# GpSimd multiplies the own rows of the node stages, and SP begins the stores of their tiles

## The chip, the cores and the metric

The kernel runs on one NeuronCore of one Trainium2 chip. The metric is the device time of one execution in microseconds; a lower one is better. The engines are named as in the profile: PE (TensorE, the matrix engine), DVE (VectorE), ACT (ScalarE), POOL (GpSimd) and SP (SyncE, which only begins transfers here). Each engine runs its own list of instructions in order; they meet at semaphores.

## The reference, cut to what matters

One layer of a graph network over 6250 nodes with 256 features, beside a linear attention over the same rows, and then a mixture of experts. The graph part has three GAT layers over 200,000 edges and a loop at every node (its own edge):

```
xn = layernorm(x)
for layer in 0, 1, 2:
    xh = (h @ W).reshape(n, heads, d)
    a_s, a_d = (xh * att_src).sum(-1), (xh * att_dst).sum(-1)
    alpha = leaky_relu(a_s[src] + a_d[dst], 0.2)      # edges and own loops
    alpha = softmax of alpha over the edges that end in dst
    out = segment_sum(xh[src] * alpha, dst) + bias
    h_new = layernorm(out) * g + b
    if layer > 0: h_new = h_new + h
    h = relu(h_new)
x = x + h + mix(xn)
x = x + experts(layernorm(x))
```

For a node, the loop's part of `out` is `xh[node] * alpha_own`: one row times one softmax weight per head. The edges' part comes from the sums that an edge stage has left in `acc`.

## The kernel before, in words

The program is a row of phases with a barrier of all engines between them: `prepare_walk` (lists of edges), `turn_weights`, then `node_phase` 0, `edge_phase` 0, `node_phase` 1, `edge_phase` 1, `node_phase` 2, `edge_phase` 2, and then `final_phase` and `experts`. The change touches `node_phase` alone, which `build` calls three times (stages 0, 1 and 2 below, by its argument `layer`). An edge stage lies between two node stages and takes over 2 ms.

A node stage works on 49 tiles (`NB`) of 128 nodes, over rings of four buffers (`TILE_RING`). For tile b in stages 1 and 2:

- SP loads the tile's projected rows (`rows`, 128x260) from memory, and in stage 2 also the previous h (`prev`). It waits for `h_ready` of tile b - 4 before (L565), which frees the buffers.
- DVE, in `gather_in`: `O = rows * own weight` (L660), `acc = acc * edge weight` (L662), `O = O + acc` (L665), `bn_stats` (L668), `bn_aggr` (L671). ACT takes the square root of the variance (L736, `std`).
- DVE, in `finish`: reciprocal (L681), (O - mean) * g (L691), * rstd + b (L695), and in stage 2 max(prev, 0) + O (L704). The last of them writes `Hn` and raises `h_ready`.
- PE transposes Hn (L793) and then projects the tile before it (L802, L803: five matmuls, two k steps of fp32 in two passes each and one bias). ACT copies the transposed tile (L747, `hT`) and takes the projection out of PSUM (L758 to L760, `extend`), and in stages 1 and 2 clears the tile's `acc` (L763).
- POOL waits for `h_ready` and stores Hn to memory (L584), waits for `ext_ready` and stores `ext` (L586), in that order, tile by tile.

In stage 0 there are no own rows: `X` is loaded and normalized (L668, L671, L681, L689).

DVE's order is written out by `step`: for tile b it takes turns between `gather_in` of tile b + 1 and `finish` of tile b, one instruction of each. So before the change the order on DVE is: L660, L681, L662, L691, L665, L695, L668, (L704), L671. Semaphore waits lie between them, as the dependences ask. ACT's order in step b is L736 of tile b + 1, L747 of tile b, L758 to L763 of tile b - 1. PE's order in step b is L793 of tile b, L802 and L803 of tile b - 1. Before it writes Hn, DVE waits until the store of Hn four tiles earlier has landed (`h_out`, L686); ACT does so for `ext` (`ext_out`, L756). At the end of the stage POOL waits for all stores.

Of the kernel before, what the change touches and what calls it, by code (L numbers as in the profile page):

```python
# [17 lines left out]
ALU = mybir.AluOpType  # L18
# [3 lines left out]
P = 128  # L22
# [3 lines left out]
NB = -(-N // P)  # L26
TAIL = N - (NB - 1) * P
NPAD = NB * P
H = 4
# [405 lines left out]
def padded_ring_rows(dram, i, slot):  # L435
    return dram[bass.ds((TILE_RING * i + slot) * P, P), :]
# [6 lines left out]
def node_phase(nc, layer, st, io, dr):  # L443
# [8 lines left out]
    with Phase(nc, f"node{layer}") as ph:  # L452
# [56 lines left out]
        hT_ready = ph.sem("hT_ready")  # L509
        projected = ph.sem("projected")  # L510
        ext_ready = ph.sem("ext_ready")
        h_out = [ph.sem(f"h_out{k}") for k in range(TILE_RING)]
        ext_out = [ph.sem(f"ext_out{k}") for k in range(TILE_RING)]
        block = ph.block()
# [13 lines left out]
        @block.sync  # L528
        def _(sp):
            if not first:  # L530
                for n, name in enumerate(("ln_g", "ln_b")):
                    sp.dma_start(vecs[:, n, :], broadcast_row(io[f"{name}{layer - 1}"])).then_inc(vecs_in, 16)
            sp.dma_start(W[:, :, :], W_dram.rearrange("(k p) o -> p k o", p=P)).then_inc(weights_in, 16)
            sp.wait_ge(bias_clear, 2)
            sp.dma_start(head_view(bias[:, 0:RW]), io[f"bias{layer}"].rearrange("(a h f) -> a h f", a=1, h=H)
                         .broadcast_to([3, H, D])).then_inc(bias_in, 16)
            sp.wait_ge(att_clear, 1)
            for n, a in enumerate((a_src, a_dst)):
                if heads == H:
                    for h in range(H):  # L540
                        o = (h * D) % P
                        sp.dma_start(att[o:o + D, h * D // P, n * H + h:n * H + h + 1],
                                     a[h:h + 1, :].rearrange("a d -> d a")).then_inc(weights_in, 16)
                else:

                    for k in range(2):
                        for h in range(H):
                            sp.dma_start(att[:, k, n * H + h:n * H + h + 1],
                                         a[0:1, k * P:(k + 1) * P].rearrange("a d -> d a")).then_inc(weights_in, 16)

            def load(i, slot, last):
                n = slice(0, TAIL) if last else slice(0, P)
                if first:
                    sp.dma_start(X[n, slot, :], ring_rows(io["x"], i, slot, last)).then_inc(loaded[slot], 16)
                if not first:
                    sp.dma_start(rows[:, slot, :], padded_ring_rows(dr["rows"], i, slot)).then_inc(loaded[slot], 16)
                if layer >= 2:
                    sp.dma_start(prev[:, slot, :], padded_ring_rows(dr["h"], i, slot)).then_inc(loaded[slot], 16)

            for slot in range(TILE_RING):  # L560
                load(0, slot, False)
            with sp.Fori(1, NB // TILE_RING) as i:
                for slot in range(TILE_RING):

                    sp.wait_ge(h_ready, TILE_RING * (i - 1) + slot + 2)  # L565
                    load(i, slot, False)
            sp.wait_ge(h_ready, NB - TILE_RING + 1)
            load(NB // TILE_RING, 0, True)

        @block.gpsimd  # L570
        def _(g):
# [6 lines left out]
            if first:  # L578
                g.memset(acc[:, :, :], 0.0).then_inc(consts, 1)

            def step(i, slot, last):
                b = TILE_RING * i + slot
                g.wait_ge(h_ready, b + 2)
                g.dma_start(padded_ring_rows(dr["xn" if first else "h"], i, slot), Hn[:, slot, :]).then_inc(h_out[slot], 16)  # L584
                g.wait_ge(ext_ready, b + 3)
                g.dma_start(padded_ring_rows(dr["rows"], i, slot), ext[:, slot, :]).then_inc(ext_out[slot], 16)  # L586

            over_ring(g, step)
            for slot in range(TILE_RING):
                n = NB // TILE_RING + (slot == 0)  # L590
                g.wait_ge(h_out[slot], 16 * n)
                g.wait_ge(ext_out[slot], 16 * n)

        @block.vector
        def _(v):
# [26 lines left out]
            if not first:  # L622
# [16 lines left out]
                for k in range(2):  # L639
                    c0.add(v.tensor_tensor(es[:, k, :, :], es[:, k, :, :], zr[:, :, :], ALU.mult))  # L640
                c0.wait()
                v.wait_ge(vecs_in, 32)

            N1 = 1 if first else 4
            N2 = 1 if first else 2 + (layer >= 2)

            def gather_in(i, slot, last):
# [6 lines left out]
                else:  # L654
                    o = O[:, slot, :]
                    oh = by_head(o)
                    a = acc[:, bass.ds(b, 1), 0:RW].rearrange("p a (h f) -> p (a h) f", h=H)[:, :, 0:D]
                    e, z = (es[:, k, bass.ds(b, 1), :].rearrange("p a h -> p (a h)").unsqueeze(2).broadcast_to([P, H, D])
                            for k in range(2))
                    ch.add(v.tensor_tensor(oh, head_view(rows[:, slot, :]), e, ALU.mult))  # L660
                    yield
                    ch.add(v.tensor_tensor(a, a, z, ALU.mult))  # L662
                    yield
                    ch.wait()
                    ch.add(v.tensor_tensor(oh, oh, a, ALU.add))  # L665
                    yield
                    ch.wait()
# [1945 lines left out]
```

## Time and profile before

| | |
|---|---|
| median of 3 runs | 7856.95 us |
| lowest and highest | 7854.21 and 7859.71 us |
| the profiled execution, its own time | 7847.88 us |
| its span, first to last instruction | 7846.2 us |
| PE busy | 4723.7 us (60%) |
| DVE busy | 5395.1 us (69%) |
| ACT busy | 1840.4 us (23%) |
| POOL busy | 5214.3 us (66%) |

The page gives the busy time of each engine over the whole span. Most of it is that of the three edge stages. The three node stages take some 110, 170 and 185 us with their starts and ends, so the shares of the page say little on them, and the trace is asked stage by stage. Stage 0 lies at about 125 to 240 us of the span, stage 1 at 2387 to 2564, stage 2 at 4700 to 4892. PEclk, the granted TensorE clock, is 0.5 at 1.2 GHz and 1.0 at 2.4 GHz; a value between them is a mean over both.

### The profile page before, as it was taken

To read this page: it belongs to the slowest core of one execution; us is meant where nothing else is said; L and a number is where in the kernel's file an instruction comes from. 1 tells how busy PE (TensorE), PEld (TensorE's weight loads), DVE (VectorE), ACT (ScalarE), POOL (GpSimd) and SP (SyncE) were. 2 spreads that over 40 slices of the span, in tenths; PEclk is the share of its full clock that TensorE was granted. 3 is DMA by queue.
4 is the path that set the end of the run, shared out by engine and by line. 5 is a ranking of instruction groups with operands and counts; after the bars stand their busy time and mean duration, and the time that the engine had idled before them with its cause. 6 is when DMAs were issued, how large, how long until landed. Compare 5 with 4: busy or idle time off the path is not lost. (4 is left out here: it accounts for less than half of the span.)

```text
span 7846.2 us, 112094 instructions
## 1 busy us (share of the span) xinstructions
PE 4723.7 (60%) x22712; PEld 3574.8 (46%) x22713; DVE 5395.1 (69%) x14589; ACT 1840.4 (23%) x6460; POOL 5214.3 (66%) x5539
## 2 busy tenths in 40 slices
PE   3466666656656366666655556466666655553686
PEld 2344444444444244444444443355555544432575
DVE  4477777777768477777777667577777776678333
ACT  1211111111103122222211104133333311114454
POOL 3677777777772777777777753777777777743333
PEclk7688888777777688888877775788888877775898
DMA  3555555555553455555544434455555544436333
GB/s 103 160 165 167 170 170 169 163 164 165 164 146 100 134 146 149 149 146 146 147 141 137 136 95 143 141 152 154 154 149 153 152 141 138 135 103 197 66 57 78
DMA packets 544968, 1106.94 MB, mean 141 GB/s; under 512 B 129378, under 2 KB 337743, under 8 KB 544227
## 3 DMA queue, kind: packets, MB, share of 16 engines
q0 software_dynamic: 274368, 731.65, 34.4%
q1 hardware_dynamic: 268883, 368.24, 15.1%
q8 instruction: 168, 2.75, 0.1%
q14 instruction: 397, 3.25, 0.1%
q10 hardware_dynamic: 1152, 1.05, 0.0%
HBM read 960.64 MB, written 148.65 MB: 141 GB/s over the span
## 5 line engine op out<-in xcount | busy, mean ns | idle before, releaser
L1108 POOL DMA_INDIRECT edges_G<-rows,edges_index x4980 | 4747.3, 953 | 1550.7 <-issue 1472.3
L1302 PE MATMUL edges_ps_o<-edges_G,edges_OH 128*128 128x264 f32 x9960 | 3211.9, 475 | 2262.9 <-DVE acc L1566 2259.5
L1302 PEld LDWEIGHTS edges_ps_o<-edges_G,edges_OH 128*128 128x128 f32 x9960 | 2211.7, 236 | 2969.8 <-DVE acc L1566 1774.7
L1548 DVE TENSOR_TENSOR edges_G<-edges_G,edges_ps_c 128x1024 f32<-128x1024 f32 x1245 | 1502.7, 1207 | 0.2 <-issue 0.2
L1566 DVE TENSOR_TENSOR acc<-acc,edges_ps_o 128x264 f32 x2490 | 1052.2, 423 | 244.6 <-DVE acc L1566 142.8
L1447 DVE TENSOR_TENSOR edges_tu<-edges_ad,edges_G 128x80 f32<-128x80 f32 x249 | 74.9, 301 | 1448.7 <-DMA edges_G<-rows,edges_index 1448.7
L1540 DVE TENSOR_TENSOR edges_OH<-edges_ps_c,relT 128x512 f32<-128x512 f32 x1245 | 844.6, 679 | 1.2 <-issue 0.6
L1145 ACT ACTIVATE edges_fade<-edges_ps_s 128x4 f32<-128x4 f32 x249 | 43.2, 174 | 2796.3 <-PE edges_ps_s L1269 2710.9
L1127 ACT ACTIVATE edges_node<-terms 128x12 bf16 x2490 | 476.5, 209 | 178.4 <-issue 124.1
L2382 POOL DMA_INDIRECT x<-experts_Y,experts_token x105 | 170.2, 1621 | 351.8 <-DVE experts_token L2517 218.5
L1135 ACT ACTIVATE edges_ps_c<-edges_diff 128x80 f32<-128x80 f32 x249 | 60.0, 241 | 1262.5 <-DVE edges_diff L1528 1261.3
L1434 DVE TENSOR_SCALAR edges_OHT<-edges_rels,lane 128x1280 bf16<-128x1280 bf16 x498 | 260.9, 566 | 0.0
L2407 PE MATMUL experts_psH<-experts_xs,experts_Wup 128*128 128x128 f32 x1680 | 213.5, 281 | 66.8 <-DVE experts_Wup L2497 65.8
L2407 PEld LDWEIGHTS experts_psH<-experts_xs,experts_Wup 128*128 128x128 f32 x1680 | 198.6, 193 | 101.5 <-issue 78.2
L586 POOL DMA_DIRECT2D rows<-node_ext x147 | 80.2, 545 | 212.8 <-ACT node_ext L760 174.5
L802 PE MATMUL node_psB<-node_Wx,node_hT 128*128 128x264 f32 x588 | 219.7, 512 | 0.0
L1260 PEld LDWEIGHTS edges_ps_s<-edges_node,edges_OHT 128*128 128x128 bf16 x4980 | 161.2, 96 | 118.9 <-issue 59.2
L1974 POOL DMA_INDIRECT xslot<-final_XH,final_slots x98 | 99.1, 1011 | 172.2 <-DVE final_slots L2154 144.1
L1260 PE MATMUL edges_ps_s<-edges_node,edges_OHT 128*128 128x12 bf16 x4980 | 161.7, 168 | 79.0 <-DVE edges_OHT L1434 63.3
L2416 PE MATMUL experts_psY<-W,experts_hT 128*128 x840 | 198.6, 379 | 0.1
L1289 PEld LDWEIGHTS edges_ps_s<-edges_dropped,edges_front 128*128 128x128 f32 x498 | 155.6, 313 | 50.1 <-issue 3.5
L2497 DVE COPY experts_Wup<-W 128x1024 f32 x105 | 94.7, 902 | 114.4 <-issue 71.6
(342 smaller groups left out, 6192.9 us busy)
## 6 DMA issues: line engine op xcount, KB each, us to landing
edges_rels<-rel SPq DMA_DIRECT2D x249, 640.0 KB
edges_G<-rows,edges_index POOLq DMA_INDIRECT x4980
xslot<-edges_blank SPq DMA_DIRECT2D x80, 650.0 KB
edges_masks<-lanes SPq DMA_DIRECT2D x249, 96.0 KB
rows<-node_ext POOLq DMA_DIRECT2D x147, 130.0 KB, 2.3
experts_X<-xslot SPq DMA_DIRECT2D x105, 130.0 KB, 2.1
node_rows<-rows SPq DMA_DIRECT2D x98, 130.0 KB, 2.1
edges_xm<-xn SPq DMA_DIRECT2D x98, 128.0 KB
```

Of the source, the lines that this page charges most:

```text
L802: pe.matmul(psB[slot % 2][:, 0:RW + H], hT[:, slot % TILE_RING, k, :], Wx[:, k, :], start=(k == 0), stop=False)
L1108: g.indirect_dma_start(G[n][:, s, 0:RW], None, dr["rows"], bass.IndirectOffsetOnAxis(index[n][:, s:s + 1], 0)).then_inc(gathered[n], 16)
L1127: ins = a.activation(node[n][:, g, :], terms[:, bass.ds(b, 1), :, :].rearrange("p a h k -> p (a h k)"), ACT.Copy)
L1260: mm = pe.matmul(ps_ad[:, s * KEPT:(s + 1) * KEPT], OHT[:, s, :], node[n][:, s // 2, :], start=True, stop=True)
L1302: mm = pe.matmul(ps_o[BANK_OF[g]][:, 0:GW], OH[:, 2 * g + j, :], G[n][:, 2 * g + j, :], start=(j == 0), stop=(j == 1))
L1434: v.tensor_scalar(OHT[:, s, :].rearrange("p s e -> p (s e)"), rels[:, c * WG * P:(c + 1) * WG * P], lane[:, 0:1], None, ALU.is_equal).then ...
L1540: v.tensor_tensor(OH[:, 4 * k:4 * k + 4, :], ps_iota.unsqueeze(1).broadcast_to([P, 4, P]), rel.unsqueeze(2).broadcast_to([P, 4, P]), ALU.i ...
L1548: v.tensor_tensor(g4[:, :, :, 0:D], g4[:, :, :, 0:D], ps_w[:, 4 * k:4 * k + 4, :].unsqueeze(3).broadcast_to([P, 4, H, D]), ALU.mult).then_ ...
L1566: v.tensor_tensor(a, a, ps_o[BANK_OF[g]][:, 0:GW], ALU.add).then_inc(added, 1)
L2382: g.indirect_dma_start(dr["x2"], bass.IndirectOffsetOnAxis(token[:, slot, :], 0), Y[:, slot, :], None, compute_op=ALU.add).then_inc(y_out, 16)
L2407: mm = pe.matmul(psH[slot % 2][:, c * P:(c + 1) * P], Wup[:, slot % 2, k, c * P:(c + 1) * P], xs[:, slot % 2, k, :], start=(k == 0), stop= ...
L2416: mm = pe.matmul(psY[slot % 2][:, 0:C], hT[:, slot % 2, c * P:(c + 1) * P], W2[:, bass.ds(e, 1), c, :].rearrange("p a o -> p (a o)"), star ...
```

## The change

DVE's first multiplication, L660, goes. In its place POOL computes the same product for every tile of stages 1 and 2, ahead of DVE by up to four tiles. It waits for the own weights once (`shares_ready`), and for each tile for its load and for the buffer O. DVE waits for POOL's result (`owned`) before the addition of L665. The stores of Hn and of ext go from POOL's queue to SP's, in all three stages. SP's loop over the tiles is written out, 49 tiles in straight line, with the store of ext two tiles behind: store Hn of b, load tile b + 4, store ext of b - 2. POOL's list is written out too. What SP and POOL wait for at the end of the stage moves to SP.

```diff
+            def store_h(b):
+                sp.wait_ge(h_ready, b + 2)
+                sp.dma_start(dr["xn" if first else "h"][b * P:(b + 1) * P, :], Hn[:, b % TILE_RING, :]).then_inc(h_out[b % TILE_RING], 16)
+
+            def store_rows(b):
+                sp.wait_ge(ext_ready, b + 3)
+                sp.dma_start(dr["rows"][b * P:(b + 1) * P, :], ext[:, b % TILE_RING, :]).then_inc(ext_out[b % TILE_RING], 16)
+
...
-            with sp.Fori(1, NB // TILE_RING) as i:
-                for slot in range(TILE_RING):
-
-                    sp.wait_ge(h_ready, TILE_RING * (i - 1) + slot + 2)
-                    load(i, slot, False)
-            sp.wait_ge(h_ready, NB - TILE_RING + 1)
-            load(NB // TILE_RING, 0, True)
+            for b in range(NB):
+                store_h(b)
+                if b + TILE_RING < NB:
+                    load((b + TILE_RING) // TILE_RING, b % TILE_RING, b + TILE_RING == NB - 1)
+                if b >= 2:
+                    store_rows(b - 2)
+            for b in (NB - 2, NB - 1):
+                store_rows(b)
+            for slot in range(TILE_RING):
+                n = NB // TILE_RING + (slot == 0)
+                sp.wait_ge(h_out[slot], 16 * n)
+                sp.wait_ge(ext_out[slot], 16 * n)
...
-            def step(i, slot, last):
-                b = TILE_RING * i + slot
-                g.wait_ge(h_ready, b + 2)
-                g.dma_start(padded_ring_rows(dr["xn" if first else "h"], i, slot), Hn[:, slot, :]).then_inc(h_out[slot], 16)
-                g.wait_ge(ext_ready, b + 3)
-                g.dma_start(padded_ring_rows(dr["rows"], i, slot), ext[:, slot, :]).then_inc(ext_out[slot], 16)
...
+            def weigh_own(b):
+                slot = b % TILE_RING
+                g.wait_ge(loaded[slot], 16 * loads * (b // TILE_RING + 1))
+                if b >= TILE_RING:
+
+                    g.wait_ge(h_ready, b - TILE_RING + 2)
+                g.tensor_tensor(by_head(O[:, slot, :]), head_view(rows[:, slot, :]),
+                                es[:, 0, b, :].unsqueeze(2).broadcast_to([P, H, D]), ALU.mult).then_inc(owned, 1)
+
+            if not first:
+                g.wait_ge(shares_ready, 1)
+                for b in range(NB):
+                    weigh_own(b)
...
                 c0.wait()
+                v.sem_inc(shares_ready, 1)
                 v.wait_ge(vecs_in, 32)
 
-            N1 = 1 if first else 4
+            N1 = 1 if first else 3
...
-                    e, z = (es[:, k, bass.ds(b, 1), :].rearrange("p a h -> p (a h)").unsqueeze(2).broadcast_to([P, H, D])
-                            for k in range(2))
-                    ch.add(v.tensor_tensor(oh, head_view(rows[:, slot, :]), e, ALU.mult))
-                    yield
+                    z = es[:, 1, bass.ds(b, 1), :].rearrange("p a h -> p (a h)").unsqueeze(2).broadcast_to([P, H, D])
                     ch.add(v.tensor_tensor(a, a, z, ALU.mult))
                     yield
                     ch.wait()
+                    v.wait_ge(owned, b + 1)
                     ch.add(v.tensor_tensor(oh, oh, a, ALU.add))
```

By the taking of turns in `step`, the order on DVE becomes: L662, L681, L665, L691, L668, L695, L671, (L704).

## Rows read from the trace of the kernel before

**Rows 1.** Instructions that write Hn, by tile; first and last start in us.

```profile
L689 DVE TENSOR_SCALAR node_Hn<-node_X,node_mv,node_rstd x49: 410/413/509, 144.3 to 231.4; 128x256 f32<-128x256 f32 x49
L695 DVE SCALAR_TENSOR_TENSOR node_Hn<-node_O,node_rstd,node_vecs x49: 475/479/485, 2410.2 to 2546.7; 128x256 f32<-128x256 f32 x49
L704 DVE SCALAR_TENSOR_TENSOR node_Hn<-node_prev,node_O x49: 402/407/424, 4723.6 to 4875.3; 128x256 f32<-128x256 f32 x49
```

**Rows 2.** Windows, stages 1 and 2: us; busy PE, PEld, DVE, ACT, POOL; PEclk, DMA, GB/s.

```profile
2413.00:2545.00 132.00, 100.91 (x322) 60.88 (x323) 117.85 (x370) 63.39 (x276) 48.57 (x90) 0.71 0.43 135
4727.00:4873.00 146.00, 118.85 (x322) 69.09 (x322) 128.24 (x413) 63.82 (x273) 48.55 (x90) 0.57 0.51 161
```

**Rows 3.** Timeline, stage 1, DVE: start us, duration us, engine, line, operation [idle before].

```profile
2436.21 0.18 DVE L671 BATCH_NORM_AGGREGATE node_mv<-node_stats 128x2 f32<-128x6 f32 x1
2436.37 0.43 DVE L660 TENSOR_TENSOR node_O<-node_rows,node_es 128x256 f32<-128x256 f32 x1
2436.75 0.16 DVE L681 RECIPROCAL node_rstd<-node_sd 128x1 f32<-128x1 f32 x1
2436.91 0.42 DVE L662 TENSOR_TENSOR acc<-acc,node_es  x1
2437.25 0.48 DVE L691 SCALAR_TENSOR_TENSOR node_O<-node_O,node_mv,node_vecs 128x256 f32<-128x256 f32 x1
...
2437.98 0.48 DVE L695 SCALAR_TENSOR_TENSOR node_Hn<-node_O,node_rstd,node_vecs 128x256 f32<-128x256 f32 x1
2438.37 0.42 DVE L668 BATCH_NORM_STATS2 node_stats<-node_O 128x6 f32<-128x256 f32 x1
2438.93 0.18 DVE L671 BATCH_NORM_AGGREGATE node_mv<-node_stats 128x2 f32<-128x6 f32 x1
```

**Rows 4.** Timeline, stage 1, a chain from one square root to the next but one.

```profile
2482.88 0.29 ACT L736 ACTIVATE node_sd<-node_mv,node_eps 128x1 f32<-128x1 f32 x1
...
2483.21 0.16 DVE L681 RECIPROCAL node_rstd<-node_sd 128x1 f32<-128x1 f32 x1 [0.41 <-ACT node_sd L736]
...
2484.44 0.48 DVE L695 SCALAR_TENSOR_TENSOR node_Hn<-node_O,node_rstd,node_vecs 128x256 f32<-128x256 f32 x1
...
2484.97 0.69 PE L793 MATMUL node_psA<-ident,node_Hn 128*128 128x128 f32 x2 [0.35 <-DVE node_Hn L695]
...
2487.35 0.40 PE L803 MATMUL node_psB<-node_bias,node_ones 3*128 3x264 bf16 x1
...
2488.62 0.29 ACT L736 ACTIVATE node_sd<-node_mv,node_eps 128x1 f32<-128x1 f32 x1
```

**Rows 5.** Timeline, stage 2, DVE: from the reciprocal to Hn.

```profile
4799.86 0.16 DVE L681 RECIPROCAL node_rstd<-node_sd 128x1 f32<-128x1 f32 x1
...
4801.82 0.41 DVE L704 SCALAR_TENSOR_TENSOR node_Hn<-node_prev,node_O 128x256 f32<-128x256 f32 x1
```

**Rows 6.** Timeline at the start of stage 0: a POOL and a DVE instruction.

```profile
125.75 10.87 POOL L579 MEMSET acc<- 128x12936 f32 x1
...
128.40 8.38 DVE L601 CAST node_parts<-node_bias 3x264 bf16<-3x264 f32 x1 [4.11 <-DMA node_bias<-in_L_gnn_bias]
136.81 0.42 DVE L603 TENSOR_TENSOR node_bias<-node_bias,node_parts 3x264 f32<-3x264 f32 x1
```

**Rows 7.** Waits in stage 0, 145 to 233 us: total us, times, longest.

```profile
DVE node_Hn L689 <- DMA xn<-node_Hn: 3.7, 8, 1.3
```

**Rows 8.** DMA issues: queue, count, KB each, median us from issue to landing.

```profile
rows<-node_ext POOLq DMA_DIRECT2D x147, 130.0 KB, 2.3
...
x<-final_Hn SPq DMA_DIRECT2D x49, 128.0 KB, 1.7
```

**Rows 9.** Timeline at the end of stage 2: the last ext and its store.

```profile
4879.95 0.39 ACT L760 ACTIVATE node_ext<-node_psB 128x260 f32<-128x260 f32 x1
...
4880.84 0.54 POOL L586 DMA_DIRECT2D rows<-node_ext  x1
```

**Rows 10.** Timeline, stage 2, SP's queue: two loads behind each other.

```profile
4724.24 0.35 SPq L556 DMA_DIRECT2D node_rows<-rows  x1
4724.77 0.34 SPq L558 DMA_DIRECT2D node_prev<-h  x1
```

More of the change, by code:

```diff
@@ L511, in node_phase @@
         ext_ready = ph.sem("ext_ready")
+        shares_ready = ph.sem("shares_ready")
+        owned = ph.sem("owned")
         h_out = [ph.sem(f"h_out{k}") for k in range(TILE_RING)]
@@ L579, in _ @@
                 g.memset(acc[:, :, :], 0.0).then_inc(consts, 1)
-            def step(i, slot, last):
-                b = TILE_RING * i + slot
-                g.wait_ge(h_ready, b + 2)
-                g.dma_start(padded_ring_rows(dr["xn" if first else "h"], i, slot), Hn[:, slot, :]).then_inc(h_out[slot], 16)
-                g.wait_ge(ext_ready, b + 3)
-                g.dma_start(padded_ring_rows(dr["rows"], i, slot), ext[:, slot, :]).then_inc(ext_out[slot], 16)
[L588 to L592, printed above, removed]
+            def weigh_own(b):
[9 more added lines that the diff above has]
+                    weigh_own(b)
         @block.vector
```

## Prediction

> **What bounds the kernel now.** The page says little here, since the change lies in three short stages. I first asked when Hn is written: first and last start over 48 steps give a tile every (231.4 - 144.3)/48 = 1.815 us in stage 0, 2.844 in stage 1 and 3.160 in stage 2 [rows 1]. All of the change's steady part is 49 tiles times a difference of such periods; 1% of a stage is 1.4 us of 7857, so even a large gain is small.
>
> Then the windows: in stage 1 DVE is busy 117.85 of 132 us, but PE too is busy 100.91, and the granted clock is 0.71, so 42% of the time lies at 2.4 GHz and 58% at 1.2. In stage 2 it is 0.57: 14% and 86% [rows 2]. So two limits have to be worked out for each stage, one per clock level.
>
> The first is DVE's own list. In a stretch where it never waits, one tile goes from L671 to L671 in 2.72 us [rows 3]. The reader is to see that an instruction begins before the one ahead has ended: a tensor_tensor of 0.42 us takes a place of 0.34 us, a scalar_tensor_tensor of 0.48 takes 0.39, L681 and L671 0.16 each. Stage 2 has L704 besides, which fills most of the 0.56 us that DVE otherwise spends from L668 to L671: some 2.82 us, an estimate.
>
> The second is a chain through three engines, at 1.2 GHz. ACT works in order, so the square root of tile b + 3 stands behind taking out and clearing tile b, that waits for PE's projection of b, which stands behind the transposes of b + 1, and these wait for Hn of b + 1, so for the square root of b + 1. The rows show it: square root at 2482.88, reciprocal at 2483.21, Hn done at 2484.92, PE from 2484.97 to 2487.75, the square root but one at 2488.62 [rows 4]. That is 0.33 + 1.71 + 0.05 + 2.78 + 0.87 = 5.74 us for two tiles, 2.87 each, which is the period of stage 1 as measured. With stage 2's 2.37 us from reciprocal to Hn done [rows 5] in the place of 1.71 it is 6.40, 3.20 each. At 2.4 GHz PE's 2.78 would be about half (an estimate), the chain 4.35, 2.2 each, and DVE bounds. So 0.58/2.87 + 0.42/2.72 gives 2.81 us a tile in stage 1 and 0.86/3.20 + 0.14/2.82 gives 3.14 in stage 2, within 0.04 us of the measured periods.
>
> **The multiplication leaves DVE.** What goes is a place of 0.38 us [rows 3], and the new order also puts L695 between L668 and L671, where DVE waited. New list: L662 0.34, L681 0.16, L665 0.34, L691 0.39, L668 0.34, L695 0.39, L671 0.16, together 2.12; the square root between L671 and L681 takes some 0.6 and only 0.50 covers it, so 2.22. That is 0.50 less than 2.72. In stage 2 L704 covers the square root: 2.45.
>
> But the chain doesn't get shorter in stage 1. From reciprocal to Hn there were L681, L662, L691, L665, L695; now there are L681, L665, L691, L668, L695: again 1.71. At 1.2 GHz the period stays 2.87, and the freed 0.65 us become DVE idle. In stage 2 L704 now waits only for L695: 0.16 + 0.34 + 0.39 + 0.34 + 0.53 + 0.41 = 2.17 for 2.37, the chain 6.20, 3.10 each.
>
> **The multiplication on POOL.** The trace has no such instruction on POOL. The nearest row is the memset, 10.87 us for 12936 elements, 0.84 ns each [rows 6], 0.22 us for 256. A product reads twice and writes once; if these passes follow each other it is 0.65 us (an estimate). I take that; the ends are 0.22 and twice 0.65. POOL has one of them per tile and no stores any more, so it isn't the bound. Its result comes in time: SP begins the load of tile b + 4 some 0.5 us after Hn of b, it lands about 2 us later, plus 0.65, while DVE wants it three rounds of over 2.2 us later.
>
> The question is what it does to DVE. While the memset runs, DVE's L601, a cast of three partitions, lasts 8.38 us, and DVE goes on 0.19 us after the memset's end [rows 6]. So a POOL instruction can keep a DVE instruction out for its whole length. L601 has one input; whether L662, L665, L691 and L695, with two inputs from SBUF, are kept out no row shows. I take it that they are (bounds: nothing, and the full hold per tile). Of 0.65 us about 0.2 then lie beside L668, L671 and L681, and 0.45 delay DVE where it has no idle time. At 2.4 GHz stage 1 goes to 2.22 + 0.45 = 2.67 from 2.72, stage 2 to 2.90 from 2.82. At 1.2 GHz the hold falls into the freed 0.65 us of idle: nothing. It comes there by timing too: it starts some 2.7 us after Hn of b, close behind Hn of b + 1, when DVE is soon to wait for the square root. Stage 1: 0.58/2.87 + 0.42/2.67 is 2.78, less 0.02 x 49 = 1 us. Stage 2: 0.86/3.10 + 0.14/2.90 is 3.07, less 0.07 x 49 = 3.5 us.
>
> The Trainium skill (SBUF — State Buffer, "SBUF: two separate sides") says that GpSimd and VectorE share one pair of ports as an exclusive lock for a whole instruction, and that an operation of VectorE with two SBUF inputs takes it against one of GpSimd that reads SBUF. The trace agrees as far as the 8.38 us of L601 go; for two inputs no run here shows it. By that rule the sum is the one above; without it, it is that of the first rival. The GPSIMD Engine Reference ("Elementwise — side-by-side cycle accounting") of the same skill gives about 2.6 cycles an element for this operation, 0.6 us for 256 by an estimate from it, and advises VectorE for it.
>
> **The start of stages 1 and 2.** POOL can start four tiles at once, 2.6 us of holds while DVE begins: about 1 us each, +2 us; ends 0 and +5.
>
> **The stores go to SP.** POOL stored Hn of b + 1 behind ext of b, which PE has late. In stage 0 DVE waits for the landing 8 times, 3.7 us [rows 7]. SP stores Hn at once, and its stores land in 1.7 us for 2.3 on POOL's queue [rows 8], so this goes: -3.7 us, ends 0 and -8 if the stumbles behind these waits go too. Each issue takes SP 0.53 us [rows 10]. Stage 0 needs three per tile, 1.6 us of 1.815; stage 2 four, 2.1 of 3.1. That fits, and what waits behind SP's wait for ext of b - 2 is the next Hn store; ext of b - 2 is projected before Hn of b exists, so it is short. The written-out lists of SP and POOL cost fetches that no row prices; four buffers cover it: 0 to +3.
>
> At the end of a stage the last ext is done at 4880.34, and POOL begins its store at 4880.84, being busy with Hn of the last tile [rows 9]. SP is free: 0.4 earlier and 0.6 faster in landing [rows 8], 1 us for each of three stages: -3 us; ends 0 and -4.
>
> **The sum.** -1 - 3.5 + 2 - 3.7 - 3 = -9.2 us. On the profiled execution's own 7847.88 this is 7838.7; that one lies 9.1 us below the median of the three runs (0.12%), outside their spread, so I carry the difference to the median: 7856.95 - 9.2 = 7847.7.
>
> **The rivals.**
> First: POOL's product doesn't keep DVE out. Then stage 1 is 0.58/2.87 + 0.42/2.22, 2.56 for 2.81, -12 us; stage 2 0.86/3.10 + 0.14/2.45, 2.99 for 3.14, -7.5 us; no loss at the starts: -26 us, 7831. For it: all rows of the hold are of a one-input cast. A denser PE that is granted 2.4 GHz more often would add a few us. Chance 0.24.
> Second, slower: the hold is longer than DVE's idle. Up to 0.85 us (0.65 idle and 0.2 beside one-input work) it costs nothing at 1.2 GHz, and the loss in stage 1 at 2.4 GHz is small. From there each 0.1 us costs 9.8 us over 98 tiles, so it is even at about 0.9 and 0.2% slower from 1.05. With 1.1 us: stage 1 3.12 for 2.81 (+15), stage 2 3.35 for 3.14 (+10), less the 4.7 of the rest: +21, 7878; with 1.3 us 7898. For it: POOL has no row of a two-input instruction. Chance 0.18.
> Third: the change doesn't do what it says; DVE waits elsewhere (clearing of acc on ACT, a later load), and the stores weren't on the path: 7857, within 4 us. Chance 0.13.
> The forecast has 0.45, with 7838 to 7858 as its own range.
>
> **How the numbers follow.** A measurement of this kernel can tell about 0.2%, 15.7 us, from no change. Faster by more (under 7841.2): most of the first rival and a tail of the forecast, 0.31. Slower by more: most of the second, 0.17. Within: 0.52. The range 7827 to 7882 leaves out a part of the first rival (clock gains) and the second beyond 1.1 us.
>
> **What would show it.** In stage 1 of the new trace tiles at 1.2 GHz still come every 2.87 us, and DVE waits for L736 before L681 where it hardly did. POOL's product lasts 0.65 us. L662, L665, L691 or L695 show durations above 0.42 and 0.48, by up to 0.5, in places where POOL works; if they don't, the first rival is right. The wait of L689 on the store in stage 0 is gone, and the last store of a stage begins within 0.1 us of the last ext. The prediction is wrong if the hold is over 0.9 us, if it falls between L681 and Hn at 1.2 GHz, or if the clock changes its shares.

## The result, and the profile of the changed kernel

| | before | changed |
|---|---|---|
| median | 7854.61 us (5 runs) | 7813.59 us (5 runs) |
| lowest and highest | 7854.21 and 7859.71 us | 7807.4 and 7818.03 us |
| profiled execution, its own time | 7847.88 us | 7807.4 us |
| its span | 7846.2 us | 7805.6 us |

The ratio is 0.9946, with a 95% interval of 0.9932 to 0.9961: the changed kernel is 0.54% faster, 41 us by the medians and 40.5 us by the two profiled executions. The prediction was 7847.7 us, 9.2 us less than the 7856.95 known then, with a range from 7827 to 7882; so it was wrong, and the time lies below its range.

Lines of the changed kernel are about 15 further on: L662, L665, L668, L671, L681, L691, L695, L704 and L689 of before are now L676, L680, L683, L686, L696, L706, L710, L719 and L704. L602 is the new product on POOL; the stores stand at L555 and L559 on SP.

First, when Hn is written in the changed kernel, to be read against [rows 1], and the windows of stages 1 and 2, against [rows 2] (columns as there):

```profile
L704 DVE TENSOR_SCALAR node_Hn<-node_X,node_mv,node_rstd x49: 411/413/415, 146.8 to 230.3; 128x256 f32<-128x256 f32 x49
L710 DVE SCALAR_TENSOR_TENSOR node_Hn<-node_O,node_rstd,node_vecs x49: 458/467/839, 2403.3 to 2528.6; 128x256 f32<-128x256 f32 x49
L719 DVE SCALAR_TENSOR_TENSOR node_Hn<-node_prev,node_O x49: 424/424/886, 4694.3 to 4840.0; 128x256 f32<-128x256 f32 x49
```

```profile
2406.00:2527.00 121.00, 87.87 (x322) 53.44 (x322) 107.91 (x321) 64.91 (x274) 29.82 (x45) 0.83 0.49 148
4697.00:4838.00 141.00, 108.26 (x324) 63.86 (x325) 122.61 (x369) 63.64 (x275) 30.72 (x45) 0.66 0.55 168
```

The steady part of a stage, from the first Hn to the last, went from 87.1 to 83.5 us in stage 0 (3.6 less), from 136.5 to 125.3 in stage 1 (11.2 less) and from 151.7 to 145.7 in stage 2 (6.0 less). That is 21 of the 40.5 us. The granted clock rose from 0.71 to 0.83 and from 0.57 to 0.66.

The other large part lies where no tile is worked on. Timeline around the end of stage 1, kernel before (start, duration, engine, line, operation, idle before it): the last projection taken out, its store, and the first instructions of the edge stage behind it.

```profile
2552.55 0.39 ACT L760 ACTIVATE node_ext<-node_psB 128x260 f32<-128x260 f32 x1
...
2553.24 0.54 POOL L586 DMA_DIRECT2D rows<-node_ext  x1 [0.87 <-ACT node_ext L760]
...
2564.68 0.33 SPq L1030 DMA_DIRECT2D edges_rels<-rel  x1
2564.70 0.55 ACT L1119 ACTIVATE edges_index<-srcT 128x20 int32<-128x20 f32 x4 [11.45 <-PEq L102]
```

The same place in the changed kernel:

```profile
2532.17 0.40 ACT L775 ACTIVATE node_ext<-node_psB 128x260 f32<-128x260 f32 x1
...
2535.41 0.32 SPq L1045 DMA_DIRECT2D edges_rels<-rel  x1
```

From the end of the last ext to the first transfer of the edge stage it was 11.74 us and is now 2.84 (I call this the gap). The same gap is 11.81 and 3.54 us behind stage 0, 11.70 and 2.82 behind stage 2: 26 us less in all.
```profile
L100 ACTq DRAIN  x1: 14/14/14, 2553.5 to 2553.5; - x1
...
L100 DVEq DRAIN  x1: 17/17/17, 2554.8 to 2554.8; - x1
...
L100 POOLq COMPARE_BRANCH  x1: 38/38/38, 2555.3 to 2555.3; - x1
L100 POOLq DRAIN  x1: 8052/8052/8052, 2555.5 to 2555.5; - x1
```

Changed kernel, end of stage 1:

```profile
L100 POOLq DRAIN  x1: 721/721/721, 2523.0 to 2523.0; - x1
...
L100 SPq DRAIN  x1: 7/7/7, 2534.6 to 2534.6; - x1
```

So a store issued at 2553.24 had landed by 2555.3, and then POOL drained for 8.05 us while every other engine stood still for it. It did so after stages 0 and 2 too (8.06 and 8.05 us). In the changed kernel POOL is through at 2523.7, ahead of the others (its 0.72 us lie over its last product, which runs from 2523.03 to 2523.65), and SP's own drain takes 7 ns.

The account of the two profiled executions: all that is ahead of stage 0 +2.6; from a stage's start to its first Hn -0.1, +0.7 and +0.3; steady parts -20.7; from the last Hn to the last ext +1.5, -2.3 and -1.2; gaps -26.0; edge stages 0 and 1 about 0; all that is behind stage 2's gap +4.7. Together -40.6, the difference of the spans. The change touches nothing ahead of stage 0: the stage starts at 124.7 us in the kernel before, at 126.5 in e13 below, which has the same code up to there, and at 126.0 to 128.5 in the others. So I take the +2.6 as scatter.

### The profile page after: what moved, and what is told of

It is laid out like the page before. It is cut to its first block and busy times, and to the rows that moved or that the text cites. A ratio compares the mean times of both kernels' runs of the same rounds, so it can differ in the third digit from the quotient of the medians.

```text
span 7805.6 us, 110848 instructions
## 1 busy us (share of the span) xinstructions
PE 4713.4 (60%) x22712; PEld 3572.6 (46%) x22713; DVE 5377.8 (69%) x14491; ACT 1841.4 (24%) x6460; POOL 5122.7 (66%) x5343
## 3 DMA queue, kind: packets, MB, share of 16 engines
q10 hardware_dynamic: 1152, 1.05, 0.0%
## 5 line engine op out<-in xcount | busy, mean ns | idle before, releaser
L602 POOL TENSOR_TENSOR node_O<-node_rows,node_es 128x256 f32<-128x256 f32 x98 | 65.9, 675 | 242.9 <-DMA node_prev<-h 103.0
L817 PE MATMUL node_psB<-node_Wx,node_hT 128*128 128x264 f32 x588 | 197.8, 469 | 0.0
```

The source lines that it names most:

```text
L817: pe.matmul(psB[slot % 2][:, 0:RW + H], hT[:, slot % TILE_RING, k, :], Wx[:, k, :], start=(k == 0), stop=False)
```

## The experiments

Each kernel is compared with the kernel before, run on the same chip in turn with it. Two theories were open. A: moving the stores gives the gap at the stage ends, and moving the product gives the steady part. B: the product gives most of it. Later the question became what the drain depends on, and what holding VectorE costs.

### e1_stores_only: the stores on SP, the product back on VectorE

```
+                    e, z = (es[:, k, bass.ds(b, 1), :].rearrange("p a h -> p (a h)").unsqueeze(2).broadcast_to([P, H, D])
+                            for k in range(2))
+                    ch.add(v.tensor_tensor(oh, head_view(rows[:, slot, :]), e, ALU.mult))
+                    yield
...
-                for b in range(NB):
-                    weigh_own(b)
```

> The changed kernel with the multiplication of the own rows put back on DVE; the stores stay on SP. Theory A (a stage whose POOL has no stores in its list ends some 9 us sooner after its last ext): three gaps from the end of the last ext to the first transfer of the edge stage of about 3 us where they were 11.7, so 26 us less, and 2 to 4 us less in stage 0; the periods of stages 1 and 2 stay at 2.84 and 3.16 us. Time 7823 to 7828 us beside 7854.6 for the kernel before. Theory B (the prediction's price of the stores, 6.7 us, holds and the rest of the gain is the product's): 7848 us, gaps of 10 us or more.

Measured: 7827.77 us, ratio 0.9960 (0.9946 to 0.9974). The gaps are 3.40, 3.09 and 3.05 us, the periods of stages 1 and 2 are 2.842 and 3.148 us, the clock 0.70 and 0.58: the steady part of stages 1 and 2 is that of before, the gaps are those of the changed kernel. Stage 0 gained its 0.065 us a tile here (1.750).

### e2_product_only: the product on POOL, the stores left there too

```
+            for b in range(NB):
+                store_h(b)
+                if b >= 2:
+                    store_rows(b - 2)
+                if not first and b + TILE_RING < NB:
+                    weigh_own(b + TILE_RING)
```

(on GpSimd, and the same lines gone from SP)

> The kernel before with the multiplication on POOL as in the change, and the stores still on POOL, in one list with it (store Hn of b, store ext of b - 2, product of tile b + 4). Theory A: the gaps at the stage ends stay at 11 to 12 us, stages 1 and 2 gain about what they gained in the change, 13 and 7 us, so 7834 to 7840 us. Theory B: the product is worth the larger part, 34 us: 7820 us. If stores delayed behind the products hold up DVE, the gain is smaller than in A and waits of DVE on stores appear.

Measured: 7843.84 us, ratio 0.9980 (0.9971 to 0.9989). Gaps 11.47, 11.69 and 11.94 us with drains of 8.05 us; periods 2.606 and 3.050, clock 0.82 and 0.69. The mirror image of e1: the steady gain without the gaps; the time is a little above theory A's 7834 to 7840. The two ratios multiply to 0.9940, and the changed kernel has 0.9946. The profiled execution, 7856.47 us, is the longest of the eleven; against the changed kernel's profile it is longer in the edge stages (5.7 and 5.0 us) and behind stage 2 (7.5), which the edit leaves alone. (This order also stores Hn before an older ext; stage 0 got 1.733 by it, without a store on SP.)

### e3_last_on_pool: only the last ext of each stage is stored by POOL

```
-            for b in (NB - 2, NB - 1):
-                store_rows(b)
+            store_rows(NB - 2)
...
+            g.wait_ge(ext_ready, NB + 2)
+            g.dma_start(dr["rows"][(NB - 1) * P:NB * P, :], ext[...]).then_inc(last_out, 16)
+            g.wait_ge(last_out, 16)
```

> The changed kernel, with one transfer of each node stage put back on POOL: the store of the last tile's ext. Theory A, in the form that POOL's last software-queue transfer is followed by some 9 us before the barrier can pass: each of the three gaps goes back to 11 to 12 us, 26 us in all, so about 7840 us. Rival: the gap depends on the number of transfers POOL has begun in the stage, or on SP being the one who waits; then one transfer changes it by 1 us at most, and the time is 7813 to 7817 us.

Measured: 7817.73 us, ratio 0.9949 (0.9936 to 0.9963); gaps 3.67, 4.17 and 3.69 us. The form of theory A by which one late transfer on POOL's queue brings the gap back is wrong. At the end of stage 1:

```profile
L100 POOLq DRAIN  x1: 130/130/130, 2543.8 to 2543.8; - x1
```

It drains behind the last ext, as before, and takes 0.13 us. So the 8.05 us are not the price of a late transfer, but of having begun many.

### e9_counts: spare transfers on POOL, of different number and size

POOL additionally stores spare data: 12 small ones (3x128 bf16) in stage 0, 48 small ones in stage 1, 48 large ones (128x264 f32) in stage 2, one at a time.

```
+            def spare_store(b):
+                to, of = ("spare", ones3) if layer < 2 else ("spare2", zeros)
+                if b:
+                    g.wait_ge(spare_out, 16 * b)
+                g.dma_start(dr[to], of[:, :]).then_inc(spare_out, 16)
```

> The changed kernel, with spare transfers begun by POOL that nobody needs: in stage 0 12 small ones (3x128 bf16), in stage 1 48 small ones, in stage 2 48 large ones (128x264 f32). The last begins before the last ext. What is read is POOL's drain at the end of each stage, 8.05 us for 98 stores and 0.13 us for one. If it goes by the number of transfers (0.08 us each): about 1.0, 3.9 and 3.9 us. If it goes by what they move: near 0.1, 0.1 and 3.9. If it is one fixed time as soon as there are more than a few: 8.05 in stages 1 and 2. The time of the whole says little here.

Measured: 7819.58 us in one execution. The drains at the ends of stages 0, 1 and 2:

```profile
L100 POOLq DRAIN  x1: 1038/1038/1038, 230.8 to 230.8; - x1
...
L100 POOLq DRAIN  x1: 3968/3968/3968, 2530.5 to 2530.5; - x1
...
L100 POOLq DRAIN  x1: 4494/4494/4494, 4847.2 to 4847.2; - x1
```

1.04, 3.97 and 4.49 us: the number counts. The amount doesn't: the 0.5 us by which 48 transfers of 135 KB take longer than 48 of 0.8 KB is POOL's last product, which was still running for 0.50 us when the drain began at 4847.20:

```profile
4847.10 0.60 POOL L603 TENSOR_TENSOR node_O<-node_rows,node_es 128x256 f32<-128x256 f32 x1 [2.53 <-DMA node_prev<-h]
```

In stage 1 the last product was done before the drain, and the changed kernel's drains of 0.72 us, without any transfer, show that a drain waits for a product. With the 0.040 to 0.046 us of a drain that has nothing to wait for and the 8.05 us of 98 transfers, each transfer costs (8.052 - 0.046)/98 = 0.0817 us; that gives 1.03 for 12, 3.97 for 48 and 0.13 for one, as measured. What POOL does in this time no run shows. The gaps stayed at 2.8 to 3.0 us, since these drains began before the last ext and were through by then: 4 us of drain cost nothing where they lie beside other work.

### e11_drain_between: drain while POOL waits anyway

The stage behind the last edges ends with such a gap too, in both kernels: 98 indirect transfers that POOL begins, and 8.15 us of drain (8.05 in the kernel before). Six drains are added between its batches:

```
                                          XH[0:tail(b), b % KEEP, :], None).then_inc(scattered[b % KEEP], 16)
+                if b % BATCH == BATCH - 1 and b < NB - 1:
+                    g.drain()
```

> The changed kernel with GpSimd's drain instruction added six times to the stage after the last edges (behind each batch of 14 indirect transfers but the last, where GpSimd waits 14 to 17 us for the next batch anyway). Nothing is left out. Theory A (the drain at a stage's end takes 0.046 us and 0.082 us for each of GpSimd's own transfers since the last drain; 1 gave 0.13, 12 gave 1.04, 48 gave 3.97 and 4.49, 98 gave 8.05): each added drain takes 1.2 us in hidden time, the drain at that stage's end falls from 8.15 to 1.2 us, and the program gets 7 us shorter (about 7806.5 against 7813.6). Theory B (the drain depends on the whole stage's transfers, drained before or not): it stays 8.1 us and the time stays or rises by up to 7.

Measured: 7820.27 us beside a kernel before of 7870.34 on this chip, ratio 0.9938 (0.9922 to 0.9955). The drain at that stage's end, in the changed kernel and in this one:

```profile
L100 POOLq DRAIN  x1: 8149/8149/8149, 7260.0 to 7260.0; - x1
```

```profile
L100 POOLq DRAIN  x1: 1187/1187/1187, 7265.2 to 7265.2; - x1
```

1.187 us for the 14 transfers since the last drain; 0.046 + 14 x 0.0817 is 1.19. So a drain only counts what has been begun since the drain before, and theory B of this run falls. The added ones are not short, though:

```profile
L1992 POOLq DRAIN  x6: 16159/18020/20178, 7064.6 to 7223.2; - x6
```

16 to 20 us against an expected 1.2. Most of that isn't draining. The drain's record begins when 12 of the 14 transfers of its batch (11 for the last drain) are still to begin, one every 1.28 us. For the first one, at 7064.64, they are these:

```profile
7064.92 0.97 POOL L1989 DMA_INDIRECT xslot<-final_XH,final_slots  x1 [0.31 <-issue]
...
7079.12 1.01 POOL L1989 DMA_INDIRECT xslot<-final_XH,final_slots  x1 [0.30 <-issue]
7097.26 1.02 POOL L1989 DMA_INDIRECT xslot<-final_XH,final_slots  x1 [17.12 <-DVE final_slots L2171]
```

From the end of the newest transfer's issue to the end of the drain it is 2.1 to 4.8 us. All six drains end 0.61 us behind the last landing: so they wait for the landing, and then take half of the 1.19 us that the formula gives for 14 transfers already landed. The next transfer began 0.8 to 14.6 us after a drain's end, so the drains held little or nothing up. What is behind stage 2's gap took 2955.1 us for 2958.9, 3.8 less where 7 were expected. The ratio's interval overlaps that of the changed kernel, so the gain in time is not shown, only the shorter drain.

### e13_before_drained: the kernel before with a drain every fourth tile

```
                 g.dma_start(padded_ring_rows(dr["rows"], i, slot), ext[:, slot, :]).then_inc(ext_out[slot], 16)
+                if slot == TILE_RING - 1:
+                    g.drain()
```

> The kernel before, its product on VectorE and all its stores on GpSimd, with one line added: GpSimd drains after every fourth tile of a node stage (8 transfers, by theory A 0.70 us each, in GpSimd's idle time). Theory A: the drain at each node stage's end, with 2 transfers left, takes 0.2 us instead of 8.05, the gaps from the last rows to the next stage's first load fall from 11.8 to 4.0 us, and the program gets some 23 us shorter (ratio 0.997, as the kernel that only moves the stores: 0.9960). Theory B (the gap belongs to who begins the stores, or the drain to the whole stage): gaps stay at 11.7, ratio 1.000 or above.

Measured: 7880.41 us, ratio 1.0014 (1.0004 to 1.0023), a miss in the time. At the end of stage 1 and in it (L588 is the added line):

```profile
L100 POOLq DRAIN  x1: 212/212/212, 2586.7 to 2586.7; - x1
```

```profile
L588 POOLq DRAIN  x12: 2390/2496/2959, 2454.0 to 2580.7; - x12
```

The last drain is as worked out (0.046 + 2 x 0.0817 = 0.21), and the gap behind stage 1 fell from 11.7 to 6.8 us. But each added drain took 2.4 to 3.0 us (up to 3.2 in stage 0), not 0.70: it waits for the landing of the newest store, and ends 0.37 us behind it. The one at 2580.7 ran until 2583.1, with the last ext done at 2581.31, so the last store began only at 2584.28, 3.0 us behind the ext; in stage 0 the drains held up the stores, and its period went from 1.815 to 2.412 us. That the gap is a drain counted in transfers is shown; as a cure it is worse than having another engine begin the stores.

### e4_no_product: what POOL's product still costs

This kernel leaves the product out: DVE adds the neighbours' sum to the own rows unweighted.

```
-                    v.wait_ge(owned, b + 1)
-                    ch.add(v.tensor_tensor(oh, oh, a, ALU.add))
+                    ch.add(v.tensor_tensor(oh, head_view(rows[:, slot, :]), a, ALU.add))
```

> Leaves out the multiplication of the own rows by their weight (DVE adds the rows as they are; neither POOL nor DVE multiplies them). It shows what the changed kernel would take if POOL's product kept nobody out. If the holds are the price that the longer DVE instructions of the new trace show (10.3 us in stage 1 and 9.1 in stage 2, of which those at 1.2 GHz may be hidden), 7795 to 7806 us, with stage 1 near 2.4 us a tile. If the holds fall into idle time altogether, the time is that of the changed kernel, 7811 to 7816 us.

Measured: 7780.95 us, ratio 0.9900 (0.9885 to 0.9915), periods 2.504 and 2.785 us. Against the changed kernel's 0.9946 the product on POOL still costs 0.46%, 36 us; by the profiled spans (7789.6 for 7805.6 us) it is 16. The profiled execution of e4 is the longest of its four and that of the changed kernel the shortest of its five, so 16 is the low end. The steady parts of stages 1 and 2 differ by 17 us in these profiles.

### e10_twice_waited: the product done twice

```
+                for n in range(2):
+                    if n:
+                        g.wait_ge(owned, 2 * b + 1)
                     g.tensor_tensor(by_head(O[:, slot, :]), ...).then_inc(owned, 1)
```

> The changed kernel with GpSimd's product of every tile done twice, one after the other: 98 more products of 0.675 us on GpSimd, nothing more on any other engine; VectorE waits for the second. GpSimd has room for it (waits of 90.5 us in the 121 us of stage 1). Theory H (what the product costs now is only the holding of VectorE's instructions with two inputs): the excess over the shortest instance in stages 1 and 2, 10.3 and 9.1 us with one product, about doubles, and the program gets 8 to 20 us longer. Theory L (VectorE also waits for the product, because it comes late): waits of the addition on the product appear, and the program gets over 20 us longer. Theory N (GpSimd's product is free): no change, within 4 us of the changed kernel. In all of them the gaps at the stage ends stay 2.8 to 3.7 us.

Measured: 7843.76 us, ratio 0.9966 (0.9953 to 0.9978), 0.2% or 16 us above the changed kernel's ratio, periods 2.844 and 3.185 us, clock 0.69 and 0.56. No wait of the addition on the product appears among the waits of either window, so theory L falls. The sum of what DVE's instructions last above the shortest of their line is 3.5 and 3.4 us in the kernel before (stages 1 and 2), 13.3 and 10.8 in the changed one, 20.1 and 17.4 here. Less the scatter of before: 9.8 and 7.4 us of holding for one product, 16.6 and 14.0 for two. That is theory H for the hold, and against theory N; the time alone doesn't settle N, since the two intervals overlap. The hold isn't all of it: stage 1's steady part is 11.2 us longer than the changed kernel's for 6.8 us more of holding. Fewer tiles run at 2.4 GHz (15 for 27), and DVE waits longer for the square root (12.0 us for 7.4).

### e6_clear_on_pool, e7_load_first, e12_both

Two small variations, and the first with e11's drains:

```
(e6) -                    a.activation(acc[...], zeros[:, :], ACT.Copy).then_inc(acc_clear, 1)
     +                        g.memset(acc[:, b - TILE_RING, :], 0.0).then_inc(acc_clear, 1)
(e7)                 sp.wait_ge(h_ready, b + 2)
     +                if b + TILE_RING < NB:
     +                    load((b + TILE_RING) // TILE_RING, ...)
                     store_h(b)
```

> The changed kernel with the clearing of acc moved from ACT to POOL (a memset of 128x264, 0.31 us, per tile). By the chain through ACT (square root, Hn, PE, taking out, clearing, square root) this shortens two tiles by 0.31 to 0.4 us where PE runs at 1.2 GHz: about 2 us in stage 1 and 6 in stage 2, ratio 0.993 to 0.994. If a memset on POOL holds DVE as the one at the start of stage 0 does, DVE's instructions get longer by up to 0.3 us per tile, 98 tiles, and it is slower than the changed kernel: ratio 0.996 to 0.998.

> The changed kernel with one thing in SP's order changed: the load of tile b + 4 goes ahead of the store of Hn of tile b. In stage 0 of the changed kernel DVE waits 8.3 us for loads, which it didn't before. If that is SP's order, most of it goes and stage 0 falls from 1.74 to some 1.70 us a tile: 2 us less, ratio 0.9940 to 0.9945, the waits on loads below 3 us. If it is the landing that is late, nothing changes.

> The kernel that clears the sums on GpSimd (0.9938 of the kernel before) together with the six added drains. If theory A holds and the two add up: 7808.5 - 7 = about 7801.5, ratio 0.993. If the clearing on GpSimd was worth nothing, the same as the kernel with the added drains alone.

Measured: e6 7808.53 us, ratio 0.9938 (0.9924 to 0.9952); e7 7812.03, 0.9944 (0.9931 to 0.9958); e12 7814.15, 0.9929 (0.9912 to 0.9946). None is told apart from the changed kernel's 0.9946 by its interval; e12 is the lowest, and 0.7% below the kernel before. In the traces e6's first theory shows all the same in stage 2: its steady part is 141.3 us in e6 and 140.8 in e12, against 145.3 to 148.5 in the changed kernel, e3, e7 and e11; in stage 1 nothing shows. e7 shows a wait that changed its name. Waits in stage 0, 145 to 230 us (total us, times, longest), the changed kernel and then e7:

```profile
DVE node_stats L683 <- DMA node_X<-in_x: 8.3, 17, 3.0
```

```profile
DVE node_rstd L697 <- ACT node_sd L752: 21.8, 43, 2.1
DVE node_stats L684 <- DMA node_X<-in_x: 3.5, 2, 3.0
```

With the load begun before the store, DVE no longer waits for it behind the first tiles, but waits longer for the square root (15.4 us in the changed kernel), and the period only goes from 1.740 to 1.717 us.

## Why the prediction was wrong

**The stage ends: the step that failed.** The prediction looked at the last ext and its store, priced the 0.4 us that POOL comes late and the 0.6 of the landing, 1 us a stage [rows 8, 9], with ends of 0 and -4 for all three, and stopped there. Measured were 8.3, 8.9 and 8.9 us a stage, 26 for 3. Of its two terms the first was about right: SP begins the last store 0.03 us behind the last ext, where POOL did 0.29 to 0.49 behind it. The second was read from another store's row ([rows 8] has final_Hn on SP beside ext on POOL). The median landing of ext's own stores in the changed kernel is no shorter on SP:

```profile
rows<-node_ext SPq DMA_DIRECT2D x147, 130.0 KB, 2.3
```

The last stores of the stages landed in 2.21, 2.03 and 2.11 us before and in 2.46, 1.77 and 1.76 now, 0.1 less in the mean and not 0.6. The rest of the gap, from that landing to the first transfer, went from 9.11, 9.41 and 9.09 us to 1.04 or 1.05, and 8.05 of that is the drain. What the prediction left out was the question of what comes next: the reader of [rows 9] should follow on to the first instruction of the next stage, 11.2 us behind that store (4880.84 to 4892.04). The waits name it in the trace of before, here from 2548 to 2566 us (total us, times, longest):

```profile
POOL edges_G L1108 <- ACT edges_index L1119: 11.6, 1, 11.6
ACT edges_index L1119 <- PEq L102: 11.4, 1, 11.4
DVE edges_eps L1410 <- PEq L102: 10.2, 1, 10.2
```

A wait of 10 to 11 us of all engines for a sequencer, three times, is some 30 us in which nothing is computed, more than all the steady terms of the sum. e1, e3, e9 and e11 show what it is: POOL's drain, 8.05 us for the 98 stores that it began. With 8 us of it a stage in the sum, nothing else altered, the forecast would have been -9.2 - 24 = -33 us, 7824.

**The multiplication off DVE: the list was right.** Without any product (e4) the tiles of stage 1 that run at 2.4 GHz take 2.240 us; the new list was worked out at 2.22. In stage 2 it is 2.535 for 2.45. The table below has the mean time from Hn to Hn, with the number of tiles, by the granted clock of that tile's own window (0.55 and less, 0.95 and more; the mixed tiles are left out):

| | stage 1, 1.2 GHz | stage 1, 2.4 GHz | stage 2, 1.2 GHz | stage 2, 2.4 GHz |
|---|---|---|---|---|
| before | 2.831 (22) | 2.731 (15) | 3.164 (38) | 2.830 (4) |
| changed | 2.759 (7) | 2.448 (27) | 3.080 (29) | 2.855 (10) |
| e4, no product | 2.583 (4) | 2.240 (25) | 2.858 (11) | 2.535 (22) |
| e10, product twice | 2.857 (24) | 2.740 (15) | 3.171 (40) | 3.050 (2) |

**The hold: the mechanism was right, its size was not.** POOL's product lasts 0.61 us in most places, 0.675 in the mean (said: 0.65), and it does keep two-input instructions of DVE out. Timeline of the changed kernel in stage 1, DVE and POOL:

```profile
2465.00 0.42 DVE L683 BATCH_NORM_STATS2 node_stats<-node_O 128x6 f32<-128x256 f32 x1
2465.13 0.61 POOL L602 TENSOR_TENSOR node_O<-node_rows,node_es 128x256 f32<-128x256 f32 x1 [1.78 <-DMA node_rows<-rows]
2465.34 0.69 DVE L710 SCALAR_TENSOR_TENSOR node_Hn<-node_O,node_rstd,node_vecs 128x256 f32<-128x256 f32 x1
...
2470.85 0.61 POOL L602 TENSOR_TENSOR node_O<-node_rows,node_es 128x256 f32<-128x256 f32 x1 [1.44 <-DVE node_Hn L710]
2470.90 0.84 DVE L676 TENSOR_TENSOR acc<-acc,node_es  x1
```

L676 takes 0.84 us for 0.42, L710 0.69 for 0.47, while L683, with one input, isn't longer. None of DVE's two-input instructions lasts over 0.49 us where it doesn't meet the product. So the first rival falls, though its period for stage 1, 2.56, came nearer to the measured 2.61 than the forecast's 2.78. But the price of 0.45 us for every tile was too high: L676 is long in 21 of 46 tiles, L680 in 10, L710 in 5, and the total is 9.8 us over 46 tiles, 0.21 each (0.16 in stage 2). Of it 3.4 us in stage 1 and 4.7 of 7.4 in stage 2 fall between the reciprocal and Hn; the prediction had named this place, at 1.2 GHz, as one that would make it wrong. The product often falls where DVE waits or runs L683, L686 and L696. At 2.4 GHz that gives 2.240 + 0.21 = 2.45, as the table has it (2.448), where 2.67 was predicted. In stage 2 the tile costs 2.855, near the predicted 2.90, but that is in part luck: e4 shows a dearer list there (2.535) and a price of the product of 0.32, of which the hold explains 0.16. At 1.2 GHz the hold was to cost nothing; e4's 2.583 and 2.858 against 2.759 and 3.080 say 0.18 and 0.22, on few tiles (4 and 11 of e4's), so it isn't settled.

The Trainium skill (SBUF — State Buffer, "SBUF: two separate sides") has GpSimd and VectorE exclude each other over shared ports for two-input operations of VectorE; the rows above agree, one-input L683 included. The same skill's GPSIMD Engine Reference ("Elementwise — side-by-side cycle accounting") led to an estimate of 0.6 us for this product, and the 0.61 of most instances agrees.

**At 1.2 GHz the period stays: nearly.** Said were 2.87 and 3.10; measured 2.759 and 3.080, from 2.831 and 3.164. The stretch from the reciprocal to the end of Hn, which was to stay 1.71 us in stage 1 and fall to 2.17 in stage 2, is 1.74 and 2.20 there (medians of the tiles at 1.2 GHz). DVE waits more for the square root (7.4 us, 16 times, in stage 1's window, for 3.1 us, 8 times), as said.

**The clock's share: named as what would make the prediction wrong, and it did.** The sum kept 42% of stage 1 at 2.4 GHz. Of the 48 tiles 15 ran wholly at 2.4 GHz before, 27 after; e2 has 24 and e4 25, e1 and e10 have 15, so it goes with the product's place and price and not with the stores. It scatters too: e11, whose stage 1 is that of the changed kernel, has 34. With before's numbers of tiles (22, 11 mixed, 15) the changed kernel's tile times would give 22 x 0.072 + 11 x 0.171 (the mixed ones) + 15 x 0.283 = 7.7 us; by this reckoning the other 3.5 of the 11.2 us in stage 1 come from tiles that changed level, which is no more than stage 1 scatters by. Why a shorter list on DVE goes with more tiles at 2.4 GHz no run here shows; that it does, e1 and e10 (15 and 15) against e2, e4 and the changed kernel show.

**Stage 0** gave -3.6 us in its steady part for -3.7, and the wait on the store is gone, as said. That the sizes agree is in part luck: DVE's waits for loads went from 1.8 to 8.3 us, and those for the square root from 23.6 to 15.4. e2 has the same gain with the stores on POOL, so it comes with the order, Hn ahead of an older ext, and not with SP. From the last Hn to the last ext it takes 1.5 us longer, so the stage up to its last ext gained 2.2 us.

**The starts** cost +0.7 and +0.3 us for +2. **The last store** begins on SP right behind the last ext, as said. The +4.7 us behind stage 2's gap have no cause that I found: that part took 2954 to 2969 us in the kernels here (2954.2 before, 2961.1 in e13 with the same code there) with no order by what they changed, so I take it as scatter. Node stages with nearly the same code also scatter: 2.562 to 2.641 us a tile in stage 1 for the changed kernel, e3, e7 and e11, 4 us in all.

So of the 31 us between forecast and result, 23 are the drain, about 16 the steady part of stages 1 and 2 (17.2 for 4.5, and the 3.5 from the last Hn to the last ext of these stages), less some 8 for what lies ahead of stage 0 (2.6) and behind stage 2 (4.7), and for stage 0 and the starts.

## What to carry to other kernels

Read the trace across the seam between two stages, from the last store to the first instruction behind it, with the sequencers' instructions: busy time doesn't show what stands there. Where POOL begins many transfers and then a stage closes, let another engine begin them, or see that POOL is through before the others. When an instruction moves to an engine that can keep another one out, count in how many tiles the two will meet, and not just how long one meeting is.

## What the runs showed of the hardware

- A drain of POOL behind transfers that have landed takes 0.046 us and 0.0817 us for each transfer that POOL has begun since its last drain, small or large, direct or indirect: 0.13 us for 1, 0.21 for 2, 1.04 for 12, 1.19 for 14, 3.97 for 48, 8.05 for 98 (one of 98 indirect ones took 8.15).
- A drain in the midst of transfers waits for the last landing and ends 0.37 us behind it with 8 transfers (e13), 0.61 us with 14 (e11), about half of what the formula gives. Its record also covers the transfers that POOL has yet to begin, and a product that still runs.
- The count doesn't go on without a limit, and where it ends no run shows. Behind the edge stages, with 1660 transfers each, the drain is 23.2 us, of which 15.0 pass until the last 12 transfers are begun; it ends 8.2 us after that, about as long as 98 take. There it lies beside other work.
- SP, with 98 stores and more begun in the same stages, drains in 7 ns.
- POOL's product of two 128x256 f32 tiles takes 0.61 us in most places and up to 0.895; a two-input instruction of DVE that meets it lasts up to 0.46 us longer (0.886 for 0.424), and a one-input one (BATCH_NORM_STATS2) doesn't.
